# A two-layer graph network with routed experts: layer 1, layer 2 and the experts in one program, the last tile's update among layer 2's first sums

## What is computed

```python
def gnn(x, edge_index, W, b, resW, resb):           # two layers
    src, dst = edges plus one loop at every node
    deg = segment_sum(ones, dst);  dis = rsqrt(deg)
    norm = dis[src] * dis[dst]
    for l in range(2):
        x_res = x
        h = x @ W[l]
        agg = segment_sum(norm[:, None] * h[src], dst) + b[l]
        x = relu(agg + x_res @ resW + resb)
    return x

x = x + gnn(layernorm(x), ...)
x = x + experts(layernorm(x))      # router: two layers, softmax, top 2 of 6; expert: three layers
```

## Time and profile before

| | us |
|---|---|
| median of 3 runs | 2022.34 |
| lowest, highest | 2022.12, 2026.24 |
| the profiled execution | 2023.09 |
| its span from first to last instruction | 2020.9 |
| PE busy | 1851.0 (92% of the span) |
| DVE busy | 1120.6 |
| ACT busy | 770.0 |
| POOL busy | 387.6 |

### The profile page before, as it was taken

One profiled execution on the slowest core, in us unless ns is written; L12 is line 12 of the kernel. 1 busy time (PEld: TensorE's weight loads), 2 busy tenths in 40 slices (PEclk: granted clock), 3 DMA queues, 4 the chain that ended last, 5 costly groups with the idle time before them and its releaser, 6 DMA issues. The chain is left out here.

```text
span 2020.9 us, 34549 instructions
## 1 busy us (share of the span) xinstructions
PE 1851.0 (92%) x11170; PEld 1131.6 (56%) x11170; DVE 1120.6 (55%) x2789; ACT 770.0 (38%) x1686; POOL 387.6 (19%) x403
## 2 busy tenths in 40 slices
PE   4448799999999999999979999999999988988896
PEld 4336555555555555555524544445444577877775
DVE  7247766666666666666514444444444566644443
ACT  2226655665566556655502222222222222222221
POOL 1680000000000000000001111121111133336564
PEclk8669799999999999999989999999999999999998
DMA  7254498899899952323455544455544566767783
GB/s 222 58 90 107 138 328 300 285 346 276 274 296 290 307 184 87 154 115 126 160 219 187 203 169 174 172 185 202 196 169 174 181 200 194 251 212 249 241 259 116
DMA packets 120764, 409.05 MB, mean 202 GB/s; under 512 B 14505, under 2 KB 74753, under 8 KB 114425
## 3 DMA queue, kind: packets, MB, share of 16 engines
q1 hardware_dynamic: 82792, 283.38, 40.2%
q0 software_dynamic: 37904, 124.85, 21.1%
HBM read 198.26 MB, written 219.86 MB: 207 GB/s over the span
## 5 line engine op out<-in xcount | busy, mean ns | idle before, releaser
L1395 PE MATMUL bank<-parts,counts 128*128 128x512 f16 x4802 | 1181.3, 379 | 12.1 <-issue 12.1
L1395 PEld LDWEIGHTS bank<-parts,counts 128*128 128x128 f16 x4802 | 426.0, 97 | 383.5 <-issue 18.1
L1557 ACT ACTIVATE counts<-bank 128x392 f16<-128x392 f32 x800 | 394.8, 497 | 312.3 <-PE bank L1473 305.5
L606 DVE TENSOR_TENSOR rows_lo<-pair_keys,iota_lo 128x2048 bf16<-128x2048 bf16 x200 | 244.9, 1225 | 239.6 <-PE bank L1473 239.4
L1473 PEld LDWEIGHTS bank<-rows_hi,rows_lo 128*128 128x128 bf16 x3200 | 229.5, 99 | 202.1 <-issue 27.3
L1473 PE MATMUL bank<-rows_hi,rows_lo 128*128 128x98 bf16 x3200 | 280.1, 211 | 9.5 <-DVE rows_hi L606 8.6
L465 POOL DMA_INDIRECT first_rows<-route_rows,route_spot_i x49 | 47.7, 973 | 833.4 <-DVE tokens L456 825.4
L606 DVE TENSOR_TENSOR rows_hi<-pair_keys,iota_hi 128x1568 bf16<-128x1568 bf16 x200 | 193.6, 968 | 0.0
L2272 DVE TENSOR_SCALAR h_t<-bank,counts 128x256 f32<-128x256 f32 x120 | 57.7, 483 | 164.3 <-PE bank L2108 120.7
L2169 ACT ACTIVATE h_t<-bank,counts 128x256 f32<-128x256 f32 x120 | 56.8, 473 | 208.2 <-PE bank L2108 154.7
L2129 PE MATMUL bank<-counts,h_t 128*128 128x256 f32 x480 | 117.9, 390 | 10.9 <-issue 6.8
(11 more groups left out here) (261 smaller groups left out, 1741.3 us busy)
## 6 DMA issues: line engine op xcount, KB each, us to landing
counts_table<-counts SPq DMA_DIRECT2D x25, 3136.0 KB, 9.7
counts<-counts_table SPq DMA_DIRECT2D x24, 3136.0 KB, 11.2
counts<-expert_pack SPq DMA_DIRECT2D x60, 898.0 KB
first_rows<-zero_rows POOLq DMA_DIRECT2D x3, 10530.0 KB, 58.1
second_rows<-zero_rows POOLq DMA_DIRECT2D x3, 10449.0 KB, 65.6
res_tile<-res_table SPq DMA_DIRECT2D x98, 128.0 KB, 6.5
first_rows<-zero_rows POOLq DMA_DIRECT2D x1, 10270.0 KB, 59.3
second_rows<-zero_rows POOLq DMA_DIRECT2D x1, 10191.0 KB, 61.6
```

The lines of the kernel that those rows point to most:

```text
L606: return nc.vector.tensor_tensor(rows, k, v, ALU.is_equal)
L1395: mm = nc.tensor.matmul(acc[:, 0:2 * dim], lhs, rhs, start=s == 0, stop=s == tiles)
L1557: nc.scalar.activation(counts[:, b, :, :].rearrange("p s (o n) -> p o s n", o=2)[:, :, :, q * QUAD:(q + 1) * QUAD], bank[4 + q % 4][:, 0:Q ...
```

## The change

Both layers and the experts become one program for each engine: `count_and_sum` and `sum_and_route` now return five functions each, and one block runs them one after the other on every engine. The rare case is the other branch of one common test, which stands ahead of both layers.

- PE: `turn` and `products` of the last tile leave the end of layer 1. Layer 2's first pair is summed in `first_sums`: chunk by chunk, seven units of the first tile and seven of the second, with the transposes behind the first chunk and the products between the halves of the second. The two units that add the tiles' own rows come last, one behind the other. PE waits for each chunk, for the two banks to be empty, and in the last chunk for the last tile's parts.
- SP: the first load of counts is issued when layer 1's last sum is done, ahead of the first rows. In front of those rows stands a wait for the residual rows in DRAM (`wait_res_stored`), which POOL did before.
- ACT: issues the store of the last tile's residual row, formerly SP's.
- Memory: layer 1's working buffers are cut out of the experts' row buffer, and those of the rare case out of `counts`.

The core of the difference, with lines that only change their indentation left out:

```diff
         def count_and_sum(update, carve):
...
                     sum_pair(pairs - 1, 0, False, last=True)
-                    update.turn(pe, tiles - 1, 0)
-                    update.products(pe, tiles - 1, 0)
...
                         update.middle_part(act, T, T % 2, kept)
+                update.store_res(act, tiles - 1, 0)
...
-                    update.store_res(sp, tiles - 1, 0)
                     for b in range(2):
                         sp.wait_ge(counts_stored[b], 16 * len(range(b, pairs, 2)))
...
                     store_zeros(pool)
-                    update.wait_stored(pool, last_kept=True)
+            return tensor, vector, scalar, sync, gpsimd
...
+        LAST_TURN_AT, LAST_PRODUCTS_AT = (0, 1), (1, 0)
...
-        def sum_and_route(update, router, work):
+        def sum_and_route(before, update, router, work):
...
                     def pair(i, j, b, last):
                         if not is_at(i, 0):
-                            if not (isinstance(i, int) and i < 2):
+                            if is_at(i, 1):
+                                sp.wait_ge(before.sums_ready, tiles)
+                            else:
                                 sp.wait_ge(update.sums_ready, 2 * i - 2)
                             sp.dma_start(counts[:, 1 - b, :, :].rearrange("p s n -> p (s n)"),
...
+                        if is_at(i, 0):
+                            return
+                        if is_at(i, 1):
+                            before.wait_res_stored(sp)
+                            for o in range(2):
+                                update.load(sp, o, o, 0, tile=tile_of(0, o))
                         update.load(sp, i * 2, 0, i, last_tile=last, tile=tile_of(i, 0))
...
+                def first_sums(pe):
+                    def unit(o, s, lhs, rhs):
+                        return nc.tensor.matmul(bank[half_bank + o][:, 0:2 * dim], lhs, rhs, start=s == 0, stop=s == tiles)
+                    for c in range(tiles // CHUNK):
+                        pe.wait_ge(chunk_back[c], 16)
+                        for o in range(2):
+                            if c == 0:
+                                pe.wait_ge(before.sums_out, tiles - 1 + (o == 0))
+                            for s in range(c * CHUNK, (c + 1) * CHUNK):
+                                if s == tiles - 1 and o == 0:
+                                    pe.wait_ge(before.high_ready, tiles)
+                                    pe.wait_ge(before.middle_ready, tiles)
+                                unit(o, s, counts[:, 1, s, o * P:(o + 1) * P], parts[:, s, :])
+                            if (c, o) == LAST_TURN_AT:
+                                before.turn(pe, tiles - 1, 0)
+                            if (c, o) == LAST_PRODUCTS_AT:
+                                before.products(pe, tiles - 1, 0)
+                    for o in range(2):
+                        unit(o, tiles, ident_h[:, :], parts[:, HELD * 2 + o, :]).then_inc(update.sums_ready, 1)
...
-                            sum_units(pe, 1 - b, i, pair_of(i), done, to, update.sums_out, update.sums_ready, first, chunk_back if first else None)
+                            sum_units(pe, 1 - b, i, pair_of(i), done, to, update.sums_out, update.sums_ready, False)
...
+        with nc.If(many == 0):
+            first = count_and_sum(first_update, carve)
+            second = sum_and_route(first_update, second_update, router, work)
+            with nc.Block() as block:
+                @block.tensor
+                def _(pe):
+                    first[0](pe)
+                    second[0](pe)
...
```

More of the change, by code:

```diff
@@ L63, with __init__ @@
 class NodeUpdate:
[L70 removed]
+    def __init__(self, nc, l, last, sb, sem, shapes, tables, scales, both_w, bias_sum, ident, turn_bank, product_bank, router=None, carve=None):
         self.router = router
@@ new lines, in gpsimd, with pair, beside @@
+            def gpsimd(pool):
+                pool.wait_ge(zeros_stored, ZEROS)
+                def pair(i, j, b, last):
+                    if is_at(i, 0) or last:
+                        return
+                    p, pj, pb = before_pair(i, j, b)
+                    router.scatter(pool, p, pb, 2)
+                by_pairs(pool, pair)
+                def beside(b):
+                    if b == 2:
+                        router.scatter(pool, LAST_PAIR - 1, 1, 2)
+                    if b == 8:
+                        router.scatter(pool, LAST_PAIR, 0, 1)
+                work.moves(pool, beside)
@@ L2486, in gnn_moe_kernel @@
         many = nc.values_load(flag[0:1, 0:1], min_val=0, max_val=1)
[L2487 to L2490, removed]
[L2491 to L2506 removed]
+        open_scope()
@@ new lines, in gnn_moe_kernel, with _ @@
+        second_update = NodeUpdate(nc, 1, True, sb, sem, (nodes, tiles, dim), tables, (dis_back[:, 1, :], dis_next), both_w, bias_sum, ident,
+                                   bank[0], bank[1], router)
+        work = expert_blocks(router, block_rows)
+        with nc.If(many == 0):
[6 more added lines that the diff above has]
+                    second[0](pe)
+                @block.vector
+                def _(dve):
+                    first[1](dve)
+                    second[1](dve)
+                @block.scalar
+                def _(act):
+                    first[2](act)
+                    second[2](act)
+                @block.sync
+                def _(sp):
+                    first[3](sp)
+                    second[3](sp)
+                @block.gpsimd
+                def _(pool):
+                    first[4](pool)
+                    second[4](pool)
@@ L2507, in gnn_moe_kernel @@
+        with nc.Else():
+            exact_degrees()
+            free_own_sems()
+            for l in range(layers):
                 messages_to_table(l)
```

760 lines of the change are left out of this document (365 added, 395 removed).

## The result

| | before | changed |
|---|---|---|
| median, us | 2024.29 (4 runs) | 2004.14 (4 runs) |
| lowest, highest | 2022.12, 2028.14 | 1998.42, 2008.14 |
| the profiled execution | 2023.09 | 1998.42 |
| its span | 2020.9 | 1996.2 |

The ratio of the runs is 0.9896, with a 95% interval of 0.9865 to 0.9928: 21 us less, between 15 and 27. Forecast were 2005.4 us and 2003.0 to 2009.5.

The account below looks back on a forecast made before the run. PE bounds the kernel except where the layers meet; there 0.95 + 21.6 + 2.26 + 0.90 = 25.7 us replaces 42.56, so 2022.34 - 16.9 = 2005.4 us, range 2003.0 to 2009.5.

Parts of the forecast that it names:

- the 12.13 us: PE's time without work before layer 2's first matmul: wait for stores, barrier and branch, all to be removed.
- The sum: PE from layer 1's last sum to the next pair: 25.7 us instead of 42.56, 16.9 us less.
- gap one: After layer 1's last sum, PE waits until DVE's add empties the first tile's bank: 0.95 us.
- gap two: Both tiles' sums end together, so the next pair's first matmul waits for the first bank to be emptied: 0.90 us.
- No wait for chunks: Reload chunks reach PE's first layer 2 sums in time: 1.7 us to spare at the first, 7.7 at the last.
- The counts: Next pair's counts load, issued behind the last chunk, lands at 1037.7 at the late end, wanted at 1038.4; costs nothing.
- The residual store: Last tile's residual row, stored by ACT about 1022.7, lands 7.0 us later as before, at 1029.7.
- The clock: PE's granted clock stays at 1.00 at the join, since the new gaps are only 0.95 and 0.90 us.
- Rival B: The clock falls once at the join, costing the products 1.74 us: 2007.1 us; chance 0.15.
- Rival D: Alternating two banks with waits keeps PE's clock at its lower level through the first sums: 2028.7 us; chance 0.03.
- Rival C: Counts or residual rows come late behind the reload and PE stalls in the next pair, 2 to 4 us: 2009; chance 0.10.
- Rival E: The join gets faster but something later, not dependent on PE, takes the time back: 2022 us; chance 0.05.

Follow-up runs that it names:

- the version with the old order: Changed kernel with PE's order as before: last tile's transposes and products, then first tile's sums, then second's; 2007.08 us, ratio 0.9926 to the kernel before.
- the repeated comparison: The changed kernel run again without an edit beside the kernel before: 2006.07 us against 2021.18, ratio 0.9924.
- both gaps filled: Changed kernel, but free bank's tile first in the first chunk, first tile closed before second's sums in the last; 2005.07 us, ratio 0.9899 to the kernel before.

## Why the prediction was right

- **Where the time is.** Right: only the join moved. The start before layer 1's first count varied from 227.3 to 234.6 us over the ten profiles and layer 1 from 783.0 to 785.7, without a side for either kernel. Layer 2 took 550.0 to 551.7 us from the next pair to the experts; up to the end of its last full pair it was 535.5 in all ten. The text let the 12.13 us go as one; the versions split them into the wait for the last store with SyncE's old order (5.9), the branch (3.4) and the block's end (2.8).
- **The sum.** Forecast 25.7, measured 25.63 in both profiles. By terms: gap one 0.95, measured 1.02; gap two 0.90, measured 0.93; transposes and products 2.26, measured 1.94 from start to start (0.22 and 1.72), which is the overestimate that the text had allowed for. Of the gaps, the 0.07 for the signal had no row behind it: PE began 0.15 us after DVE's add, both times (1011.23 and 1011.38; 1035.84 and 1035.99). The 100 units make the rest, 21.7 against 21.6.
- **No wait for chunks.** Right; and the version with the old order shows that there was room even for a last chunk asked for some six microseconds sooner.
- **The counts.** Mis-sized, on the safe side: I took the late end, 25.0 us after layer 1's last sum, with 0.7 us to spare. It landed 21.7 us after it, with 3.9 to spare. The load did not wait for the last chunk's landing to start moving: from there, 1024.4, it took 7.7 us, and in the version where it came behind the reload 10.2.
- **The residual store.** Mis-sized, and with a wrong reason: I took 7.0 us "as before", though the counts now went ahead of it on the other queue. It took 12.0, because its small packets took turns with the big ones of the counts; I had counted the traffic, not the turns. It cost nothing, and in part that is luck. SyncE went on at 1031.78, and the first residual row landed 2.0 us later, 2 us ahead of DVE's add at 1035.88. That is 23.4 us after layer 1's last sum, even sooner than the text's 24 to 27, since the counts, behind which it had put the rows, came 3.3 us sooner than it took them.
- **The clock.** Right: 1.00 throughout. Rival B did not come, but its mechanism is real: the version with the old order shows it. Rival D, the Trainium skill's rule on cycling through banks, found nothing to hold on to: seven and seven in two banks ran at 0.216 us per sum and a clock of 1.00.
- **Rival C** did not come; the version with the counts behind the rows shows its price for one operand, 0.7 us.
- **Rival E.** Refuted within the noise: the repeated comparison gives 15.4 us (11 to 20) of less time for 15.7 to 16.9 us of shorter join. The first comparison's 21 us have an interval of 15 to 27, which holds the same gain; the profiled span's 24.7 us were 16.9 of join and otherwise the luck of one execution (6.3 in the experts' stage, 1.4 in layer 1, 1.0 at the start, less 0.9 in layer 2).

## What to carry to other kernels

A block's end costs what its slowest wait costs, and that can be a small store behind a big reload: ask which engine really needs the data, and let that one wait. Where a program can go on with data that is already there, put the leftover of the old stage among the new stage's work, and look for the other half's work to cover each emptying of a bank. When a total varies by ten microseconds, measure a change of two in the stretch of the trace where it lies.

## What was not expected of the hardware

- A store of 128 KB on ACT's queue took 4.7 us to land with no counts moving, and 9.6, 11.0, 12.0 and 12.0 us when 3136 KB of counts had been issued on SyncE's queue 2.9, 3.4, 4.6 and 4.6 us ahead of it (the versions with the old order and with both gaps filled, and the changed kernel twice). Its packets of 1 KB moved one for one with the counts' packets of 24 KB: 106 and 100 in six microseconds. The Trainium skill, "DMA: Bandwidth & Descriptors", section "Queues, rings and completion order", has a DMA engine go round-robin between its queues; these rows agree. The same section says that a completion signal lands only after the earlier writes of its DMA engine, across queues; no run here tests that, as the store's data itself came late.
- PE came past a branch 3.7 us after SyncE did; without the branch, 0.2 us after it.
- The same gaps did not make the clock fall at the same place. Behind gaps of 1.90 and 0.47 us the four products took 3.62, 2.62, 3.06, 3.07 and 1.98 us in five profiles; in the last of them the clock fell only behind a further 2.80 us of idle time. In the changed kernel's order it stayed at 1.00 behind gaps of 0.93 and 1.02 us, and behind one of 1.64 us in the version with the counts behind the rows.
